# Attention stage of a two-layer time-mix and expert kernel: TensorE's order within a step changes, with ScalarE's and VectorE's after it

## The chip, the cores and the metric

The kernel runs on one core of one Trainium2 chip. Its five engines, TensorE (PE), VectorE (DVE), ScalarE (ACT), GpSimd (POOL) and the sync engine (SP), run their own instruction streams and meet at semaphores. The metric is the device time of the whole kernel in microseconds. Before the change it is 1264.72 us, the median of three runs (1261.82, 1264.72, 1269.57).

## The reference

The input `h` has 4 sequences of 2048 tokens with 256 features. Two time-mix layers run over it, then a residual sum is normalised, then a mixture of experts (8 experts, 2 per token) and another normalised sum follow.

```python
def _time_mix_layer(x, ln_w, ln_b, Wk, Wv, Wr, Wo):
    normed = _layer_norm(x, ln_w, ln_b)
    k = jnp.einsum('btd,ed->bte', normed, Wk)
    v = jnp.einsum('btd,ed->bte', normed, Wv)
    r = jax.nn.sigmoid(jnp.einsum('btd,ed->bte', normed, Wr))
    kv = k * v
    def step(state, kv_t):
        state = DECAY * state + (1.0 - DECAY) * kv_t
        return (state, state)
    _, states = jax.lax.scan(step, init, jnp.swapaxes(kv, 0, 1))
    y = r * jnp.swapaxes(states, 0, 1)
    return x + jnp.einsum('btd,ed->bte', y, Wo)
...
x = _layernorm(x + attention(x))      # both layers; the "finished rows"
gate_out = x @ Wg.T; top 2 of 8 experts, softmax over the two
x = _layernorm(x + sum of the two experts' gated MLPs, weighted)
```

## The kernel before, in words

The kernel has three phases: attention, experts, final normalisation. Only the attention phase is touched. It works on 16 chunks of 512 tokens (`CHUNKS`), each as 4 tiles of 128 tokens (`Q`). Features lie in two halves of 128 (`DC`). Every matrix product is made of three: high part by high part, high by low, low by high. So ScalarE writes a rounded high part of each operand (`x_hi`, `y_hi`) and VectorE or GpSimd the rest (`x_lo`, `y_lo`).

The phase is a software pipeline written out by hand. Each engine has a function `step(s, half, j)`, and in step s it holds four stages of different chunks: layer 1 of chunk s, layer 2 of chunk s-1, the end of the attention of chunk s-2 (residual sum `z`, its normalisation into `x1`), and the routing of chunk s-3 (transposes of the finished rows `x1`, the gate product, the choice of experts, the scatter of slots). `run` (L279 to L286) unrolls steps 0 to 5 and 14 to 19 and puts steps 6 to 13 in a hardware loop of two steps per pass. The order of the calls in `step` is the order of the instructions on the engine; nothing else schedules them. An instruction waits at the head of its engine's queue, and all behind it wait with it.

Names that matter:
- TensorE, `step` at L924: `project(l, s, n, e, j)` makes k, v and r of layer l for feature half e (6 groups of 6 matmuls for both halves); `rows2` transposes layer 2's normalised input `normed1` into the two banks `tp`; `output2` is layer 2's output product; `rows3` transposes finished rows `x1` into the same `tp`; `gates` multiplies them by the router's weights; `transpose(0, s + 1, ...)` is layer 1's input of the next chunk, again in `tp`. The two `tp` banks are shared by three users, so each of them waits until the last one has been read: `x_lo` (L638) for the layers' inputs, `keep_x1T` (L417) for the finished rows.
- ScalarE, `step` at L433: `normalize` (L382), `x_hi` (L389), `keep_k` (L395), `gate_r` (L402), `y_hi` (L409), `keep_x1T` (L417).
- VectorE, `step` at L770: `residual1` (L745), `norm_stats` (bn_stats L624, bn_aggr L630, `ve` L632, `nm` L633), `recur` (`kv` L685, the scan L692, the carry L695), `x_lo` (L638), `residual2` (`z`, L765, with its own `norm_stats`), `choose` (L705 to L722), `place` (up to the cast into `slot_u`, L737).
- GpSimd, `step` at L561: `rstd` (L532, L534) turns `ve` and `nm` into the factors of a normalisation, `gated` (L298) multiplies state and gate into `y`, `y_lo` (L305) is its low part, and the scatters (L78) are indirect DMAs that it issues, 8 per step from step 4 on. Its order is untouched.
- TensorE's last work in a step is layer 1's output product (L876 to L878) in two halves; the second one overwrites a bank from which `place` of the same step has to read first, so it waits for `slot_u`.

Of the kernel before, what the change touches and what calls it, by code (L numbers as in the profile page):

```python
# [41 lines left out]
DC = D // P  # L42
# [22 lines left out]
def at(s, n):  # L65

    return isinstance(s, int) and s == n
# [103 lines left out]
def attention_phase(nc, h, w_att, ln_wb, w_gate, w_ffn, x_src, x_acc, slot_list, kept):  # L171
    ident, w_raw_all, base, table = kept.ident, kept.w_raw, kept.base, kept.table
    pairs, slot_u, s_sc = kept.pairs, kept.slot_u, kept.s_sc
    with ExitStack() as ctx:
# [191 lines left out]
        def _(act):  # L366
# [38 lines left out]
            def y_hi(l, n, e):  # L405
                act.wait_ge(s_y[l], n * 2 + e + 1)
                if within(n, 1, CHUNKS):
                    act.wait_ge(s_po[l], n * 2)
                nc.scalar.activation(yh[l][:, e, :], y[l][:, e, :], ACT.Copy).then_inc(s_yh[l], 1)  # L409

            def keep_x1T(s):

                for dc in range(DC):
                    act.wait_ge(s_pt[2], s * 2 + dc - 5)
                    if within(s, 4, CHUNKS + 2):
                        act.wait_ge(s_g, s - 3)
                    nc.scalar.activation(x1T[:, dc, :], tp[dc][:, :], ACT.Copy).then_inc(s_x1T, 1)  # L417
# [15 lines left out]
            def step(s, half, j):  # L433
                layer1, layer2 = within(s, 0, CHUNKS - 1), within(s, 1, CHUNKS)
                if layer1:
                    for e in range(DC):
                        if e == 1 and layer2:
                            if within(s, 2, CHUNKS):
                                act.wait_ge(s_pt[1], s * 2 - 2)
                            normalize(1, xr, normed[1], s - 1, s_n[1])  # L440
                        if at(s, 0):
                            keep_k(0, s, e, j, None, 0)
                        elif at(s, 1):
                            keep_k(0, s, e, j, s_kv[0], 2)
                        else:
                            keep_k(0, s, e, j, s_kv[1], s * 2 + e - 3)
                        gate_r(0, s, e, j)
                elif layer2:
                    act.wait_ge(s_pt[1], s * 2 - 2)
                    normalize(1, xr, normed[1], s - 1, s_n[1])  # L450
                if at(s, 0):
                    x_hi(0, 1)
                if at(s, CHUNKS):
                    keep_x1T(s)
                if layer2:
                    x_hi(1, s - 1)
                if at(s, CHUNKS):
                    normalize3(s, half, j)
                if layer1:
                    for e in range(DC):  # L460
                        y_hi(0, s, e)
                if at(s, 0):
                    split_weights(1)
                    act.wait_ge(s_biassb[1], 2)
                if within(s, 3, CHUNKS + 2) and not at(s, CHUNKS) and not at(s, CHUNKS + 1):
                    keep_x1T(s)
                if within(s, 1, CHUNKS - 2):
                    act.wait_ge(s_pt[0], s * 2 + 2)
                    normalize(0, x_in[:, 1 - j, :, :], normed[0], s + 1, s_n[0])
                if layer2:  # L470
                    if at(s, CHUNKS):
                        keep_k(1, s - 1, 0, j, s_kv[1], 2 * s - 3)
                    else:
                        keep_k(1, s - 1, 0, j, s_kv[0], s * 2 + 1)
                if within(s, 2, CHUNKS + 1) and not at(s, CHUNKS):
                    normalize3(s, half, j)
                if layer2:
                    gate_r(1, s - 1, 0, j)
                if within(s, 1, CHUNKS - 2):
                    x_hi(0, s + 1)  # L480
                if layer2:
                    if at(s, CHUNKS):
                        keep_k(1, s - 1, 1, j, s_kv[1], 2 * s - 2)
                    else:
                        keep_k(1, s - 1, 1, j, s_kv[0], s * 2 + 2)
                    y_hi(1, s - 1, 0)
                if within(s, 3, CHUNKS + 2):
                    act.wait_ge(s_gap, s - 2)
                    if within(s, 5, CHUNKS + 2):
                        act.wait_ge(s_sc[1 - j], (half - 2 + j) * SCAT)  # L490
                    nc.scalar.activation(pairs[1 - j][:, :, 0, 1], gap[:, :], ACT.Sigmoid)
                    nc.scalar.activation(pairs[1 - j][:, :, 1, 1], gap[:, :], ACT.Sigmoid, scale=-1.0).then_inc(s_prob, 1)
                if layer2:
                    gate_r(1, s - 1, 1, j)
                    if at(s, CHUNKS):
                        keep_x1T(s + 1)
                    y_hi(1, s - 1, 1)
# [114 lines left out]
        def _(dve):  # L612
# [157 lines left out]
            def step(s, half, j):  # L770
                layer1, layer2 = within(s, 0, CHUNKS - 1), within(s, 1, CHUNKS)
                if layer2:
                    residual1(s, j)
                    norm_stats(1, xr, s - 1)
                    if not at(s, CHUNKS):
                        add_input(s, j)
                if at(s, CHUNKS):
                    residual2(s, j)
                if layer1:
                    for e in range(DC):  # L780
                        recur(0, s, e, j)
                if at(s, 0):
                    x_lo(0, 1)
                    keep_bias(1)
                    low_weights(1)
                if layer2:
                    x_lo(1, s - 1)
                if within(s, 1, CHUNKS - 2):
                    dve.wait_ge(s_x[1 - j], half * 16 + 16 * (1 + j))
                    norm_stats(0, x_in[:, 1 - j, :, :], s + 1)  # L790
                if at(s, CHUNKS):
                    add_input(s, j)
                if within(s, 2, CHUNKS + 1) and not at(s, CHUNKS):
                    residual2(s, j)
                if at(s, CHUNKS):
                    choose(s - 3)
                    for e in range(DC):
                        recur(1, s - 1, e, j)
                        gated(dve, 1, s - 1, e)
                        y_lo(dve, 1, s - 1, e)  # L800
                if within(s, 3, CHUNKS + 2) and not at(s, CHUNKS):
                    choose(s - 3)
                if layer2 and not at(s, CHUNKS):
                    recur(1, s - 1, 0, j)
                if within(s, 1, CHUNKS - 2):
                    x_lo(0, s + 1)
                if within(s, 3, CHUNKS + 2):
                    place(s - 3, half, j)
                if at(s, EARLY + 2):
                    dve.wait_ge(s_base, EARLY + 1)  # L810
                    big_table(nc, dve, kept)
                if layer2 and not at(s, CHUNKS):
                    recur(1, s - 1, 1, j)
# [5 lines left out]
        def _(pe):  # L819
# [104 lines left out]
            def step(s, half, j):  # L924
# [14 lines left out]
                if at(s, CHUNKS):  # L939

                    output2(s, j)
                    rows3(s, j, s_xl[0], 2 * s)
                    rows2(s, ((s_x1T, s * 2 - 4),))
                    gates(s, s_res, s * 2)
                    project(1, s, s - 1, 0, j)
                elif at(s, CHUNKS + 1):
                    rows3(s, j, s_xl[1], 2 * s - 2)
                    output2(s, j)
                    gates(s, s_slot, s - 3)
                elif at(s, CHUNKS + 2):  # L950
                    rows3(s, j, s_x1T, 2 * s - 6)
                    gates(s, s_slot, s - 3)
                else:
                    if layer2:
                        rows2(s, ((s_xl[0], s * 2 + 2),))
                    if within(s, 2, CHUNKS):
                        output2(s, j)
                    if within(s, 3, CHUNKS):
                        rows3(s, j, s_xl[1], s * 2)
                    if layer2:  # L960
                        project(1, s, s - 1, 0, j)
                    if at(s, 3):
                        pe.wait_ge(s_wg, 16)
                    if within(s, 3, CHUNKS):
                        gates(s, s_res, s * 2)
                if within(s, 1, CHUNKS - 2):
                    pe.wait_ge(s_n[0], s + 2)

                    if within(s, 1, 2) and isinstance(s, int):
                        pe.wait_ge(s_xl[1], 2 * s)  # L970
                    else:
                        pe.wait_ge(s_x1T, s * 2 - 4)
                    transpose(0, s + 1, normed[0])
                if layer2:
                    project(1, s, s - 1, 1, j, (0, 1))
# [569 lines left out]
```

## Time and profile before

| | |
|---|---|
| Median of three runs | 1264.72 us (1261.82 to 1269.57) |
| Profiled execution: its time, its span | 1267.21 us, 1265.4 us |
| Mean granted clock of TensorE | 0.956 |
| PE busy, share of the span | 1103.8 us, 87% |
| DVE | 926.9 us, 73% |
| POOL | 858.0 us, 68% |
| ACT | 656.5 us, 52% |
| PE busy from 30 to 440 us (attention) | 361.05 of 410.00 us |
| POOL busy there | 290.78 us |

Times are microseconds from the start of the span. The attention takes the first 555 us or so. A row of the time-ordered view is a start, a duration, the engine, the line of the kernel, the operation, and its output and inputs, with a count if several equal ones are merged; behind it in brackets stands how long the engine had been idle, and what released it.

### The profile page before, as it was taken

How to read it: one execution, taken by the hardware profiler on the slowest of the kernel's cores; microseconds unless marked ns; L12 is line 12 of the kernel's file. 1: busy time of each engine (PE TensorE's matmuls, PEld its weight loads, DVE VectorE, ACT ScalarE, POOL GpSimd, SP SyncE). 2: the span in 40 equal slices, each digit the busy share in tenths (PEclk: the TensorE clock that was granted, in tenths of full speed). 3: DMA queues.
4: the chain of work that ended last, by engine and by line, in shares of the span. 5: the costliest groups of instructions: out<-in, count | busy, mean ns of one | idle time of the engine just before them, and what ended most of it. 6: DMA issues, size and time to landing. Idle time of an engine off the chain costs nothing. (4 is left out here: it accounts for less than half of the span.)

```text
span 1265.4 us, 23767 instructions
## 1 busy us (share of the span) xinstructions
PE 1103.8 (87%) x7172; PEld 988.0 (78%) x7172; DVE 926.9 (73%) x1973; ACT 656.5 (52%) x1091; POOL 858.0 (68%) x696
## 2 busy tenths in 40 slices
PE   6899888988888889748999999999999999999910
PEld 5778777777777777636888888888889999999910
DVE  5678888888888887745776666666667888888737
ACT  4455555555455554324554454444555666566618
POOL 3355777777777777666666776666677676777634
PEclk9899999999999999859999999999999999999965
DMA  4011111111111111157656666656668898998559
GB/s 150 17 51 58 48 48 51 51 50 50 50 50 50 50 51 34 34 129 185 160 139 147 161 158 154 143 137 157 151 157 224 238 237 227 238 246 229 134 167 381
DMA packets 80662, 164.20 MB, mean 130 GB/s; under 512 B 27424, under 2 KB 45600, under 8 KB 80352
## 3 DMA queue, kind: packets, MB, share of 16 engines
q1 hardware_dynamic: 49248, 126.16, 31.8%
q0 software_dynamic: 31360, 37.38, 15.7%
q8 instruction: 26, 0.43, 0.2%
q14 instruction: 28, 0.23, 0.1%
HBM read 118.01 MB, written 45.49 MB: 129 GB/s over the span
## 5 line engine op out<-in xcount | busy, mean ns | idle before, releaser
L1163 POOL DMA_INDIRECT x_acc<-fy_sb,pair_out x142 | 284.7, 2005 | 152.9 <-DVE fy_sb L1264 76.9
L1319 PE MATMUL fring<-fxh,fw_hi 128*128 128x256 f32 (+1 forms) x816 | 265.3, 325 | 4.0 <-DVE fxl L1255 1.9
L1321 PE MATMUL fring<-fxh,fw_lo 128*128 128x256 f32 (+1 forms) x816 | 265.3, 325 | 0.0
L1320 PE MATMUL fring<-fxl,fw_hi 128*128 128x256 f32 (+1 forms) x816 | 265.0, 325 | 0.0
L1182 ACT ACTIVATE fw_hi<-w_raw 128x1024 fp32r<-128x1024 f32 x153 | 161.1, 1054 | 149.0 <-PE fy L1362 132.4
L1235 DVE TENSOR_TENSOR fw_lo<-w_raw,fw_hi 128x1024 fp32r<-128x1024 f32 x153 | 186.5, 1219 | 17.8 <-ACT fw_hi L1182 16.5
L88 POOL DMA_INDIRECT xg<-x_src,pair_in x142 | 159.8, 1125 | 43.3 <-issue 42.7
L78 POOL DMA_INDIRECT slot_list<-pairs,slot_u x128 | 140.1, 1095 | 47.6 <-issue 30.9
L1319 PEld LDWEIGHTS fring<-fxh,fw_hi 128*128 128x128 f32 x816 | 153.7, 188 | 18.0 <-issue 4.1
L1360 PE MATMUL fy<-fw_hi,gh 128*128 128x256 f32 x568 | 163.7, 288 | 0.9 <-issue 0.9
L1321 PEld LDWEIGHTS fring<-fxh,fw_lo 128*128 128x128 f32 x816 | 153.8, 189 | 13.3
L1320 PEld LDWEIGHTS fring<-fxl,fw_hi 128*128 128x128 f32 x816 | 153.8, 188 | 13.2
L865 PE MATMUL ring<-xh,w_hi 128*128 128x512 f32 x384 | 158.9, 414 | 3.1 <-DVE xl L638 2.9
L1362 PE MATMUL fy<-fw_hi,gl 128*128 128x256 f32 x568 | 159.5, 281 | 1.1 <-issue 1.1
L1361 PE MATMUL fy<-fw_lo,gh 128*128 128x256 f32 x568 | 159.5, 281 | 0.4 <-issue 0.4
L866 PE MATMUL ring<-xl,w_hi 128*128 128x512 f32 x384 | 153.4, 400 | 0.0
L867 PE MATMUL ring<-xh,w_lo 128*128 128x512 f32 x384 | 153.3, 399 | 0.0
L1244 DVE TENSOR_TENSOR gated<-fring,silu 128x512 f32<-128x512 f32 x142 | 98.2, 691 | 72.4 <-PE fring L1321 62.6
L1195 ACT ACTIVATE gh<-gated 128x512 fp32r<-128x512 f32 x142 | 89.6, 631 | 83.6 <-DVE gated L1244 77.9
L298 POOL TENSOR_TENSOR y<-state,r_sb 128x512 f32<-128x512 f32 x62 | 80.2, 1293 | 70.7 <-DVE state L692 67.0
L1361 PEld LDWEIGHTS fy<-fw_lo,gh 128*128 128x128 f32 x568 | 108.4, 191 | 1.2 <-issue 1.2
L409 ACT ACTIVATE yh<-y 128x512 fp32r<-128x512 f32 x64 | 40.5, 632 | 132.4 <-POOL y L298 131.8
(148 smaller groups left out, 2378.8 us busy)
## 6 DMA issues: line engine op xcount, KB each, us to landing
w_raw<-w_ffn SPq DMA_DIRECT2D x153, 512.0 KB
x_in<-h SPq DMA_DIRECT2D x16, 512.0 KB, 3.3
x_src<-x SPq DMA_DIRECT2D x16, 512.0 KB
x_acc<-x SPq DMA_DIRECT2D x16, 512.0 KB
acc<-x_acc SPq DMA_DIRECT2D x16, 512.0 KB, 7.7
out<-o SPq DMA_DIRECT2D x16, 512.0 KB, 6.8
xg<-x_src,pair_in POOLq DMA_INDIRECT x142
x_acc<-fy_sb,pair_out POOLq DMA_INDIRECT x142
```

Source lines behind the costliest of these rows:

```text
L88: nc.gpsimd.indirect_dma_start(kept.xg[j][:, q, :], None, x_src, bass.IndirectOffsetOnAxis(kept.pair_in[j][:, q, 0:1].bitcast(U32), 0)).th ...
L865: nc.tensor.matmul(out, hi, xh[l][:, dc, :], start=dc == 0, stop=False)
L866: nc.tensor.matmul(out, hi, xl[l][:, dc, :], start=False, stop=False)
L1163: nc.gpsimd.indirect_dma_start(x_acc, bass.IndirectOffsetOnAxis(pair_out[j][:, q, 0:1].bitcast(U32), 0), y[j][:, q, :], None, compute_op=A ...
L1182: nc.scalar.activation(w_hi[:, j, low:high], w_raw[:, j, low:high], ACT.Copy).then_inc(s_whi[i], 1)
L1235: nc.vector.tensor_tensor(w_lo[:, j, low:high], w_raw[:, j, low:high], w_hi[:, j, low:high].bitcast(F32), ALU.subtract).then_inc(s_wlo[i], 1)
L1319: nc.tensor.matmul(out, hi, rows_hi, start=dc == 0, stop=False)
L1320: nc.tensor.matmul(out, hi, rows_lo, start=False, stop=False)
L1321: last = nc.tensor.matmul(out, lo, rows_hi, start=False, stop=dc == DC - 1)
L1360: nc.tensor.matmul(out, a, hi, start=hc == 0, stop=False)
L1361: nc.tensor.matmul(out, a, lo, start=False, stop=False)
L1362: last = nc.tensor.matmul(out, c, hi, start=False, stop=hc == HC - 1)
```

## The change

It reorders calls in three of the `step` functions and adjusts the waits that protect the shared `tp` banks. No instruction is added or taken away. In steps 3 to 15 TensorE's order behind layer 1's projections was: layer 2's transposes, layer 2's output, finished rows' transposes, layer 2's projections of the first half, gates. It becomes: finished rows' transposes, layer 2's output, layer 2's transposes, gates, layer 2's projections of the first half. In steps 1 and 2, which have no finished rows to transpose, the output (step 2) comes ahead of the transposes. On ScalarE the copies of the finished rows come ahead, and the two `y_hi` of layer 1 stand around layer 2's `x_hi`. On VectorE layer 2's `x_lo` moves behind `norm_stats` of the next chunk of layer 1.

```diff
--- before.py
+++ after.py
@@ -450,19 +450,20 @@
                     normalize(1, xr, normed[1], s - 1, s_n[1])
                 if at(s, 0):
                     x_hi(0, 1)
-                if at(s, CHUNKS):
+                if within(s, 3, CHUNKS):
                     keep_x1T(s)
+                if layer1:
+                    y_hi(0, s, 0)
                 if layer2:
                     x_hi(1, s - 1)
                 if at(s, CHUNKS):
                     normalize3(s, half, j)
                 if layer1:
-                    for e in range(DC):
-                        y_hi(0, s, e)
+                    y_hi(0, s, 1)
                 if at(s, 0):
                     split_weights(1)
                     act.wait_ge(s_biassb[1], 2)
-                if within(s, 3, CHUNKS + 2) and not at(s, CHUNKS) and not at(s, CHUNKS + 1):
+                if at(s, CHUNKS + 2):
                     keep_x1T(s)
                 if within(s, 1, CHUNKS - 2):
                     act.wait_ge(s_pt[0], s * 2 + 2)
@@ -783,11 +784,11 @@
                     x_lo(0, 1)
                     keep_bias(1)
                     low_weights(1)
-                if layer2:
-                    x_lo(1, s - 1)
                 if within(s, 1, CHUNKS - 2):
                     dve.wait_ge(s_x[1 - j], half * 16 + 16 * (1 + j))
                     norm_stats(0, x_in[:, 1 - j, :, :], s + 1)
+                if layer2:
+                    x_lo(1, s - 1)
                 if at(s, CHUNKS):
                     add_input(s, j)
                 if within(s, 2, CHUNKS + 1) and not at(s, CHUNKS):
@@ -951,25 +952,25 @@
                     rows3(s, j, s_x1T, 2 * s - 6)
                     gates(s, s_slot, s - 3)
                 else:
-                    if layer2:
-                        rows2(s, ((s_xl[0], s * 2 + 2),))
+                    if within(s, 3, CHUNKS):
+                        rows3(s, j, s_xl[0], s * 2 + 2)
                     if within(s, 2, CHUNKS):
                         output2(s, j)
-                    if within(s, 3, CHUNKS):
-                        rows3(s, j, s_xl[1], s * 2)
                     if layer2:
-                        project(1, s, s - 1, 0, j)
+                        if within(s, 3, CHUNKS):
+                            rows2(s, ((s_x1T, s * 2 - 4),))
+                        else:
+                            rows2(s, ((s_xl[0], s * 2 + 2),))
                     if at(s, 3):
                         pe.wait_ge(s_wg, 16)
                     if within(s, 3, CHUNKS):
                         gates(s, s_res, s * 2)
+                    if layer2:
+                        project(1, s, s - 1, 0, j)
                 if within(s, 1, CHUNKS - 2):
                     pe.wait_ge(s_n[0], s + 2)
 
-                    if within(s, 1, 2) and isinstance(s, int):
-                        pe.wait_ge(s_xl[1], 2 * s)
-                    else:
-                        pe.wait_ge(s_x1T, s * 2 - 4)
+                    pe.wait_ge(s_xl[1], s * 2)
                     transpose(0, s + 1, normed[0])
                 if layer2:
                     project(1, s, s - 1, 1, j, (0, 1))
```

TensorE in one pass of the loop, behind layer 1's projections. The names in square brackets are the semaphores waited for. Before:

```order
L823 MATMUL tp<-ident,normed 128x128 [waits xl_ready0,normed_1]
L823 MATMUL tp<-ident,normed 128x128 x7
L876 MATMUL ring<-w_hi,yh 128x256 [waits r_ready0,yl_ready1,yh_ready1]
...
L823 MATMUL tp<-ident,x 128x128 [waits xl_ready1,x1_ready]
L823 MATMUL tp<-ident,x 128x128 x7
L865 MATMUL ring<-xh,w_hi 128x512 [waits kv_ready0,xl_ready1,xh_ready1]
...
L912 MATMUL out_0<-wg,x1T 128x8 [waits residual_ready,x1T_ready]
L912 MATMUL out_0<-wg,x1T 128x8 x7
L823 MATMUL tp<-ident,normed 128x128 [waits x1T_ready,normed_0]
```

And with the change, where line numbers are one higher:

```order
L824 MATMUL tp<-ident,x 128x128 [waits xl_ready0,x1_ready]
L824 MATMUL tp<-ident,x 128x128 x7
L877 MATMUL ring<-w_hi,yh 128x256 [waits r_ready0,yl_ready1,yh_ready1]
...
L824 MATMUL tp<-ident,normed 128x128 [waits x1T_ready,normed_1]
L824 MATMUL tp<-ident,normed 128x128 x7
L913 MATMUL out_0<-wg,x1T 128x8 [waits residual_ready,x1T_ready]
L913 MATMUL out_0<-wg,x1T 128x8 x7
L866 MATMUL ring<-xh,w_hi 128x512 [waits kv_ready0,xl_ready1,xh_ready1]
...
L824 MATMUL tp<-ident,normed 128x128 [waits xl_ready1,normed_0]
```

The finished rows' transposes (`tp<-ident,x`) and the output have changed places with layer 2's transposes (`tp<-ident,normed`, waiting for normed_1), and the gates (out_0<-wg,x1T) now stand ahead of layer 2's projections.

VectorE in the second step of the loop's pass, from layer 1's carry to the statistics of `z`. Before:

```order
L695 COPY carry<-state 128x1
L638 TENSOR_TENSOR xl<-tp,xh 128x512 x2
L624 BN_STATS stats<-x_in 128x6 x4
L630 BN_AGGR mv<-stats 128x2 x4
L632 TENSOR_SCALAR ve<-mv 128x4
L633 TENSOR_SCALAR nm<-mv 128x4
L765 TENSOR_TENSOR z<-ring,u 128x512 x2
L624 BN_STATS stats<-z 128x6 x4
```

With the change:

```order
L696 COPY carry<-state 128x1
L625 BN_STATS stats<-x_in 128x6 x4
L631 BN_AGGR mv<-stats 128x2 x4
L633 TENSOR_SCALAR ve<-mv 128x4
L634 TENSOR_SCALAR nm<-mv 128x4
L639 TENSOR_TENSOR xl<-tp,xh 128x512 x2
L766 TENSOR_TENSOR z<-ring,u 128x512 x2
L625 BN_STATS stats<-z 128x6 x4
```

`xl` of layer 2 has moved behind the five groups of the next chunk's statistics and stands directly ahead of `z`.

## Rows read from the trace of the kernel before

**Rows 1.** TensorE's waits from 119 to 476 us: total, times, longest (us).

```profile
PE out L876 <- DVE slot_u L737: 17.4, 11, 1.9
PE tp L823 <- DVE xl L638: 16.1, 11, 1.6
PE tp L823 <- ACT normed L382: 13.2, 10, 1.8
```

**Rows 2.** Time order, TensorE in step 12: start, duration, operation, idle time before.

```profile
378.62 0.39 PE L865 MATMUL ring<-xh,w_hi 128*128 128x512 f32 x1
...
388.93 1.10 PE L823 MATMUL tp<-ident,normed 128*128 128x128 f32 x8 [1.73 <-ACT normed L382]
...
394.49 1.06 PE L823 MATMUL tp<-ident,x 128*128 128x128 f32 x8 [1.59 <-DVE xl L638]
395.31 0.48 PE L865 MATMUL ring<-xh,w_hi 128*128 128x512 f32 x1
...
399.69 1.85 PE L912 MATMUL out<-wg,x1T 128*128 128x8 f32 x16
...
410.24 0.38 PE L876 MATMUL out<-w_hi,yh 128*128 128x256 f32 x1 [1.84 <-DVE slot_u L737]
```

**Rows 3.** Time order, VectorE in step 12.

```profile
379.86 1.29 DVE L745 TENSOR_TENSOR xr<-out,x_in 128x512 f32<-128x512 f32 x2 [0.43 <-issue]
...
393.05 1.29 DVE L638 TENSOR_TENSOR xl<-tp,xh 128x512 fp32r<-128x512 f32 x2
394.26 1.40 DVE L624 BATCH_NORM_STATS2 stats<-x_in 128x6 f32<-128x256 f32 x4
...
396.24 1.23 DVE L632 TENSOR_SCALAR ve<-mv 128x4 f32<-128x4 f32 x1
...
408.55 1.64 DVE L737 CAST slot_u<-slot_f 128x8 uint32<-128x8 f32 x1
```

**Rows 4.** Time order, GpSimd in step 12.

```profile
394.89 1.29 POOL L298 TENSOR_TENSOR y<-state,r_sb 128x512 f32<-128x512 f32 x1
396.14 1.29 POOL L305 TENSOR_TENSOR yl<-y,yh 128x512 fp32r<-128x512 f32 x1
...
401.43 1.05 POOL L532 TENSOR_TENSOR rs<-ve,neg_half 128x4 f32<-128x4 f32 x1
...
408.88 1.27 POOL L305 TENSOR_TENSOR yl<-y,yh 128x512 fp32r<-128x512 f32 x1
```

**Rows 5.** Time order, VectorE in step 15, `ve` of z and the gates' first reader.

```profile
493.71 1.32 DVE L632 TENSOR_SCALAR ve<-mv 128x4 f32<-128x4 f32 x1
...
497.64 0.19 DVE L705 COPY g<-out 128x32 f32<-128x32 f32 x1 [2.55 <-PE out L912]
```

**Rows 6.** Time order, GpSimd in step 15, two products in a row.

```profile
492.44 2.54 POOL L305 TENSOR_TENSOR yl<-y,yh 128x512 fp32r<-128x512 f32 x2
```

**Rows 7.** Time order, TensorE in steps 1, 2 and 3.

```profile
50.15 0.48 PE L865 MATMUL ring<-xh,w_hi 128*128 128x512 f32 x1 [2.91 <-DVE xl L638]
...
76.61 0.48 PE L865 MATMUL ring<-xh,w_hi 128*128 128x512 f32 x1 [0.21 <-issue]
...
82.24 1.09 PE L823 MATMUL tp<-ident,normed 128*128 128x128 f32 x8 [1.18 <-ACT normed L382]
...
104.83 0.47 PE L865 MATMUL ring<-xh,w_hi 128*128 128x512 f32 x1
```

**Rows 8.** Time order, GpSimd's `yl` of layer 1, steps 1, 2 and 3.

```profile
49.96 1.29 POOL L305 TENSOR_TENSOR yl<-y,yh 128x512 fp32r<-128x512 f32 x1
...
76.45 1.29 POOL L305 TENSOR_TENSOR yl<-y,yh 128x512 fp32r<-128x512 f32 x1
...
103.80 1.28 POOL L305 TENSOR_TENSOR yl<-y,yh 128x512 fp32r<-128x512 f32 x1
```

**Rows 9.** Stretches: bounds, length, each engine's busy time, PEclk (granted clock), DMA share, GB/s.

```profile
33.00:38.00 5.00, 5.00 (x26) 4.94 (x25) 2.44 (x4) 0.00 (x0) 0.00 (x0) 0.57 0.00 0
50.00:56.00 6.00, 5.86 (x19) 4.62 (x20) 1.98 (x11) 2.98 (x6) 3.71 (x5) 0.72 0.00 0
```

## The prediction

> **What bounds the kernel now.** The views were read in this order: the page, the waits of TensorE in the attention stage, then the time-ordered rows of TensorE, VectorE and GpSimd for single steps. Only the attention stage changes, in its steps 1 to 15, so the question is what sets the length of a step there. Three waits stop TensorE once per step, together 46.7 us over 11 steps: for layer 2's normalised rows, for the low parts of layer 2's input (`xl`), and for the slots [rows 1]. The change is aimed at the first two. Whether they are worth anything depends on the third, because a wait that ends later in the same step takes up what the earlier ones give back.
>
> Step 12 is the step I work out; it starts at 378.62, with its first matmul, and ends some 1.5 us after the slots. TensorE waits 1.73 us for the normalised rows, 1.59 for `xl`, and 1.84 for the slots [rows 2]. The slots come from VectorE (the cast of slot_u, which ends at 408.55 + 1.64 = 410.19 [rows 3]). So the step ends by a chain VectorE, GpSimd, ScalarE, VectorE, in which TensorE has 1.84 us of spare time. The reader is to see that GpSimd is nearly always at work there, and that some VectorE operations do not run beside it: `ve`, four elements per partition, takes 1.23 us and ends at 397.47, where GpSimd's `yl` ends at 396.14 + 1.29 = 397.43 [rows 3, 4]. In step 15 `ve` takes 1.32 us, to 495.03, and two products of GpSimd in a row end at 494.98 [rows 5, 6]. The cast of the slots starts 0.33 us before a product of GpSimd at 408.88 and ends 0.04 after it [rows 3, 4]. I read this as a hold: VectorE waits until GpSimd pauses, and a GpSimd instruction that follows on the last without a gap keeps it.
>
> **The change, part by part, in steps 4 to 14 (11 steps).**
> TensorE's reordering. The transposes of finished rows and the output now stand ahead of the transposes of layer 2, so 394.49 - 1.59 - 388.93 = 3.97 us of work lie where the 1.73 us wait was, and that wait is covered. Its price is nothing, and so would be its gain as long as the slots end the step.
>
> VectorE's reordering. `x_lo` of layer 2 (two subtractions, 1.29 us as a pair [rows 3]) moves behind norm_stats of the next chunk. Its statistics start at 393.05 instead of 394.26, and `ve` at 393.05 + (396.24 - 394.26) = 395.03. At that moment GpSimd's product `y` runs (394.89 to 396.18) and `yl` follows from 396.14 without a gap [rows 4]. If the hold works as above, `ve` ends at 397.47 as before: the 1.2 us that it started earlier are lost. `x_lo` then runs where `z` stood, from 397.45 to 398.74, and TensorE's projections of layer 2 start at 398.8 instead of 395.31, 3.5 us later. The gates, 1.7 us (their row's 1.85 [rows 2], less the last one's overlap with what follows), now stand ahead of them, so the net delay of TensorE is 1.8 us, which its 1.84 us of spare time just pays. The cost falls elsewhere: `z`, its statistics and its `ve` come 1.2 us later. GpSimd used that `ve` at 401.43 without having waited [rows 4], so part of the 1.2 is hidden; bounds for the slots are 0 and 1.2 us, and I take 0.5, since the `yl` at 408.88 that the cast waits for hangs on two parallel chains, of which one only moves.
>
> TensorE's clock. The idle times of a step, now 1.7 and 1.6 us, become one: the wide matmuls, the moved output included, are done by 388.93 - 1.73 + 3.97 = 391.2, the transposes and gates by 393.7 (0.82 and 1.7 us), and the projections start at 398.8, after 5.1 us of nothing [rows 2]. In the trace of before the granted clock was 0.72 over 6.0 us after the 2.91 us wait of step 1, and 0.57 over 5.0 us after another wait at the start of the stage [rows 7, 9]; that is the 1.2 GHz level for part of the time, and a loss of 6.0 x 0.28 = 1.7 us and 5.0 x 0.43 = 2.15 us. I expect such a fall in most steps and take 1.9 us each. TensorE then ends the step, 1.9 us late. But most of this comes back: when TensorE ends a step, VectorE's next step, whose first addition now starts 1.24 us after the step does [rows 3], starts up to 1.2 to 1.7 us earlier against it, and with it all that TensorE waits for later. What stays is between 0.5 us (the slots' chain alone) and 1.0 (a fall that costs 2.4). I take 0.6: 11 x 0.6 = **6.6 us**.
>
> ScalarE's reordering puts the two copies of x1T ahead and layer 2's `x_hi` between the two `y_hi`. The wait for GpSimd's product that `y_hi` has there covers them, and a 5.1 us wait of TensorE covers a late `x_hi`. Without that cover the price would be a pair of such operations, 1.29 us as VectorE's pair, a step. I take nothing.
>
> **Steps 1 to 3.** Here GpSimd has no scatters, a step is shorter, and TensorE is close to being the bound. `ve` lands inside a `yl` of GpSimd in each of them. Step 1: that `yl` ends at 49.96 + 1.29 = 51.25 [rows 8]; `nm` and `x_lo` follow, to about 52.7, and TensorE, which started at 50.15, starts at 52.75: **+2.6**. Step 2: `yl` ends at 77.74, `x_lo` at 79.2, the projections start at 79.3 instead of 76.61, and the 1.18 us wait at 82.24 absorbs part [rows 7, 8]: 1.5, plus 1.9 for a fall of the clock, since this idle time gets about as long as the 2.91 us one of step 1: **+3.4**. Step 3: `yl` ends at 105.08 [rows 8], projections at 106.5 instead of 104.83, less 1.7 for the gates moved ahead: 0 without a fall of the clock, 2 with one; **+1.0**.
>
> **Step 15.** It has no norm_stats of a next chunk, and `x_lo` stays where it was. The gates come earlier than the projections, and VectorE waits 2.55 us for them [rows 5]. Bounds 0 and -2.55; I take **-1.5**, because the projection that follows is needed too.
>
> Sum: 6.6 + 2.6 + 3.4 + 1.0 - 1.5 = +12.1 us. The stages after the attention do not change. Against the profiled execution (span 1265.4, time 1267.21) that is 1279.3; it lies 2.5 us above the median of the three runs (1264.72), and against that the sum is **1277 us**, my prediction, 1.0% slower. Less than 1% (12.6 us) is about what cannot be told from no change.
>
> **A rule weighed against the rows.** Everything above hangs on `ve` losing twice, to `y` and then to `yl`. The rows show `ve` of steps 12 and 15 losing to a product that began at nearly the same moment, and the cast losing to one that began later [rows 3 to 6]. The Trainium skill, SBUF — State Buffer, section "A bandwidth-pool intuition that's wrong (but worth ruling out)", has the port pair of VectorE and GpSimd as an exclusive lock, and the blocked side as going on about 115 ns after the holder's end. The trace agrees on the lock; read strictly, the rule lets `ve` in between `y` and `yl`, and the sum by it would be the first rival's.
>
> **The rivals.**
> 1. *`ve` is let in between `y` and `yl`.* It ends at about 396.3, `x_lo` at 397.7, and `z` starts 0.2 us later than before: nothing in steps 4 to 14, and the clock's fall is paid by the spare time. Steps 1 to 3 keep their +7.0 and step 15 its -1.5: +5.5, 1270 us. For it: the products are two instructions with a boundary. Against it: the cast that started 0.33 us before its product and lost. Chance 0.25.
> 2. *The other side: faster.* If `ve` reaches the port before `y` does, at 394.89, it is not held: in step 12 it comes 0.14 us too late, and that is the point which decides. `x_lo` would then end at 396.4, TensorE would start at 396.5 with the gates behind it, 0.5 us ahead of now, and `nm`, `z` and the slots' products would come up to 1.2 us earlier. At 0.65 us a step that gives -7, with 3 lost in steps 1 to 3 and -1.5 in step 15: -5.5, 1259 us; with all 1.2 us a step, -12. Against it: `ve` and `y` both follow the same scan of VectorE at fixed distances, so the 0.14 us repeat from step to step. Chance 0.07.
> 3. *The clock costs more.* If each fall costs 2.4 us or more and VectorE's lead does not make up for it, steps 4 to 14 lose 1.1 to 1.5 us each, and steps 1 to 3 lose 9: about +20, 1285 us. For it: the clock fell after both of the long waits shown, and the new wait is longer than either [rows 7, 9]. Chance 0.15.
>
> My own case has 0.53. Nearly half of it lies over +12.6 us.
>
> **Numbers.** Slower by over 1%: 0.53 x 0.45 + 0.15 = 0.39, rounded to 0.40. Faster by over 1% needs nearly the most that rival 2 can give, and I leave 0.07 for it and for what I have not seen. Within 1%: 0.53. The range goes from 1262, which cuts off most of rival 2, to 1287, a little over rival 3.
>
> **What would show it.** In the changed kernel's trace: no wait of TensorE for layer 2's normalised rows; a wait of 4 to 5.5 us before layer 2's first projection, put down to `xl`; `ve` of the next chunk's statistics taking 2 us or more, up to the end of `yl`; a lower granted clock over the attention stage than now; steps 4 to 14 longer by some 0.6 us; step 1 longer by 2.6. If `ve` takes 0.2 us, rival 2 holds; if it takes 1.3, rival 1. The prediction is wrong if the slots' chain gets shorter by a way that I have priced at nothing, ScalarE's order above all.

## The result, and the profile after

The changed kernel takes **1282.99 us** in the median (1281.87 to 1286.32, 4 runs), the kernel before 1263.27 in the same comparison (4 runs). The ratio is 1.0149, 95% interval 1.0118 to 1.0179: slower by 1.5%. The forecast was 1277, range 1262 to 1287. The profiled run took 1281.92.

From the page of the changed kernel, its span and its busy times:

```profile
span 1280.2 us, 23759 instructions
PE 1118.7 (87%) x7172; PEld 1008.4 (79%) x7172; DVE 932.2 (73%) x1973; ACT 662.0 (52%) x1091; POOL 863.0 (67%) x696
```

Its waits in steps 4 to 14, the first row TensorE's only one there (total, times, longest):

```profile
PE ring L866 <- issue: 47.0, 11, 4.7
```
```profile
DVE slot L730 <- PE out L986: 11.2, 11, 1.4
```

Against [rows 1]: three waits of TensorE, 46.7 us together, have become one of 47.0. The view puts it down to "issue" and not to `xl`; that `xl` ends it is seen in the rows of single steps. TensorE did not gain any time by the merger. The second row is new: VectorE now waits for TensorE's ranks of the tokens (L986) before it can make the slots, so TensorE ends the step.

Time order in step 12 of the changed kernel (it starts at 394.82): TensorE, VectorE, GpSimd.

```profile
407.00 1.03 PE L824 MATMUL tp<-ident,normed 128*128 128x128 f32 x8
407.87 1.85 PE L913 MATMUL out<-wg,x1T 128*128 128x8 f32 x16
414.10 0.77 PE L866 MATMUL ring<-xh,w_hi 128*128 128x512 f32 x1 [4.38 <-issue]
```
```profile
395.17 1.29 DVE L746 TENSOR_TENSOR xr<-out,x_in 128x512 f32<-128x512 f32 x2 [0.43 <-PE out L879]
...
410.35 2.38 DVE L633 TENSOR_SCALAR ve<-mv 128x4 f32<-128x4 f32 x1
412.65 0.16 DVE L634 TENSOR_SCALAR nm<-mv 128x4 f32<-128x4 f32 x1
412.72 1.28 DVE L639 TENSOR_TENSOR xl<-tp,xh 128x512 fp32r<-128x512 f32 x2
413.92 1.27 DVE L766 TENSOR_TENSOR z<-ring,u 128x512 f32<-128x512 f32 x2
```
```profile
410.21 1.27 POOL L298 TENSOR_TENSOR y<-state,r_sb 128x512 f32<-128x512 f32 x1
411.43 1.27 POOL L305 TENSOR_TENSOR yl<-y,yh 128x512 fp32r<-128x512 f32 x1
```

The reader is to see the lock in these three fences. `y` begins 0.14 us before `ve`; `yl` follows it at once and ends at 411.43 + 1.27 = 412.70; `ve`, four elements per partition, begins at 410.35 and ends at 412.73. It lost to both. `xl` ends at 414.00, and the projections of layer 2 start 0.1 us later.

The stretches around the wait, for [rows 9] (columns as there), first the idle one and then most of the eighteen projections:

```profile
408.70:414.10 5.40, 1.02 (x11) 0.96 (x10) 5.20 (x13) 0.65 (x2) 4.80 (x6) 0.84 0.01 0
414.10:419.10 5.00, 5.00 (x12) 3.94 (x13) 4.40 (x26) 2.88 (x6) 3.70 (x6) 0.50 0.01 0
```

At 0.50, the 1.2 GHz level, a projection matmul takes 0.43 us instead of 0.23. The eighteen take 420.68 - 414.10 = 6.6 us; before they took 431.97 + 0.23 - 427.76 = 4.4 in step 13. The whole of steps 4 to 14 ran at a granted clock of 0.90 after and 1.00 before:

```profile
125.00:497.00 372.00, 325.00 (x1850) 279.37 (x1849) 303.48 (x807) 185.97 (x352) 274.04 (x254) 0.90 0.13 47
```
```profile
119.00:476.00 357.00, 310.33 (x1851) 261.67 (x1850) 295.20 (x804) 182.28 (x352) 273.62 (x253) 1.00 0.14 49
```

**Where the time went**, from the starts of the steps in both traces:

| | before | after | difference | forecast |
|---|---|---|---|---|
| steps 4 to 14 | 356.9 | 371.9 | +15.1 | +6.6 |
| step 1 | 26.4 | 29.6 | +3.2 | +2.6 |
| step 2 | 26.3 | 30.1 | +3.8 | +3.4 |
| step 3 | 28.9 | 27.8 | -1.1 | +1.0 |
| step 15, to layer 2's output behind it | 35.1 | 32.9 | -2.2 | -1.5 |

Together +18.8, beside 19.7 between the medians. The spans differ by 14.8 only: what follows the attention took 3.7 us longer in the profiled run of before, which lay above its median.

### The profile page after: what moved, and what is told of

It reads as the page before. It is cut to its first block and busy times, and to the rows that moved or that the text cites. A ratio compares the mean times of both kernels' runs of the same rounds, so it can differ in the third digit from the quotient of the medians.

```text
span 1280.2 us, 23759 instructions
## 1 busy us (share of the span) xinstructions
PE 1118.7 (87%) x7172; PEld 1008.4 (79%) x7172; DVE 932.2 (73%) x1973; ACT 662.0 (52%) x1091; POOL 863.0 (67%) x696
## 5 line engine op out<-in xcount | busy, mean ns | idle before, releaser
L1164 POOL DMA_INDIRECT x_acc<-fy_sb,pair_out x142 | 292.4, 2059 | 142.2 <-DVE fy_sb L1265 78.4
L866 PE MATMUL ring<-xh,w_hi 128*128 128x512 f32 x384 | 169.0, 440 | 55.5 <-issue 50.1
L867 PE MATMUL ring<-xl,w_hi 128*128 128x512 f32 x384 | 163.4, 425 | 0.0
L868 PE MATMUL ring<-xh,w_lo 128*128 128x512 f32 x384 | 162.5, 423 | 0.0
L866 PEld LDWEIGHTS ring<-xh,w_hi 128*128 128x128 f32 x384 | 80.2, 209 | 73.9 <-issue 56.7
L1196 ACT ACTIVATE gh<-gated 128x512 fp32r<-128x512 f32 x142 | 89.6, 631 | 83.6 <-DVE gated L1245 83.6
L1250 DVE TENSOR_TENSOR gl<-gated,gh 128x512 fp32r<-128x512 f32 x142 | 97.3, 685 | 15.4 <-ACT gh L1196 15.4
```

What stands on the lines that cost most here:

```text
L866: nc.tensor.matmul(out, hi, xh[l][:, dc, :], start=dc == 0, stop=False)
L867: nc.tensor.matmul(out, hi, xl[l][:, dc, :], start=False, stop=False)
L868: last = nc.tensor.matmul(out, lo, xh[l][:, dc, :], start=False, stop=dc == DC - 1)
L1164: nc.gpsimd.indirect_dma_start(x_acc, bass.IndirectOffsetOnAxis(pair_out[j][:, q, 0:1].bitcast(U32), 0), y[j][:, q, :], None, compute_op=A ...
```

## The experiments

The theory: the time is lost by one swap, VectorE's `x_lo` behind norm_stats, because `ve` is held through `y` and `yl`; TensorE pays with a wait, and then with its clock. The rivals: TensorE's new order costs by itself; the clock costs nothing that the slots' chain would not cost; the hold is something else. Times are medians, with the kernel before in the same batch.

**Undo VectorE's part in the changed kernel** (e1_xlo_back).

```diff
+                if layer2:
+                    x_lo(1, s - 1)
                 ...
                     norm_stats(0, x_in[:, 1 - j, :, :], s + 1)
-                if layer2:
-                    x_lo(1, s - 1)
```

> The changed kernel with VectorE's order alone undone: layer 2's x_lo stands ahead of norm_stats of the next chunk again; TensorE's and ScalarE's new orders stay. My reading (hold): x_lo no longer waits behind ve, TensorE finds xl ready about when the gates end, its wait of 4.4 us a step and the fall of the clock (2.1 us) are gone, steps 4 to 14 fall from 33.8 to about 32.3 us, steps 1 to 3 and 15 gain some 3 us over before: 1258 us, range 1252 to 1264. Rival (TensorE's new order itself costs, for instance through the shared tp banks): stays over 1272. Rival (the slots' chain is untouched and nothing else moves): 1263, as before the change.

Measured: 1258.98 (before 1261.45), ratio 0.999 (0.9974 to 1.0005). All of the loss is gone, by this one swap. The granted clock is 1.00 again from 125 to 480 us. TensorE's waits, 125 to 520 us:

```profile
PE out L877 <- DVE slot_u L738: 15.7, 11, 1.5
PE tp L824 <- ACT normed L382: 13.4, 11, 1.3
PE ring L866 <- DVE z L766: 7.6, 10, 0.9
```

The long wait for `xl` is gone here and nothing clear of the noise is gained: the slots end the step, as in [rows 1]. In the two profiled runs steps 4 to 14 take 352.1 us instead of 356.9 and steps 1 to 3 take 83.6 instead of 81.6. So TensorE's and ScalarE's orders cost nothing, and are worth little at most.

**Only VectorE's part, in the kernel before** (e3_dve_only).

> The kernel before with VectorE's reordering alone: x_lo of layer 2 behind norm_stats of the next chunk, TensorE and ScalarE as before. Hold theory: x_lo ends 4.2 us later, TensorE keeps its wait for the normalised rows and waits about 5 us for xl with the gates still behind it, the clock falls: 35.5 us a step instead of 32.4, +34 in steps 4 to 14 and +5 in steps 1 to 3: 1295 to 1307. Rival (the lateness comes from TensorE's new order, in which layer 2's transposes are later): under 1270.

Measured: 1340.34 (before 1261.45), ratio 1.0624 (1.0607 to 1.064), 33 us above the top of what was expected. From 125 to 520 us:

```profile
PE tp L823 <- DVE xl L638: 58.4, 10, 6.1
```
```profile
DVE g L705 <- PE out L912: 57.5, 10, 6.5
```

In TensorE's old order the gates stand behind the projections that wait for `xl`. So each of the two engines waits for the other: TensorE 6 us for `xl`, then VectorE 6 us for the gates, whose copy is the head of its work on slots. I had priced only the first. The change's new order of TensorE is what keeps VectorE's swap from costing four times as much.

**`x_lo` between the statistics and `ve`** (e2_ve_behind_xlo): norm_stats calls it after its aggregation.

```diff
+                if between is not None:
+                    between()
                 ...
-                    norm_stats(0, x_in[:, 1 - j, :, :], s + 1)
-                if layer2:
+                    norm_stats(0, x_in[:, 1 - j, :, :], s + 1, lambda: x_lo(1, s - 1))
+                elif layer2:
                     x_lo(1, s - 1)
```

> The changed kernel with x_lo of layer 2 between the bn_aggr and the ve and nm of the next chunk's statistics, so that x_lo stands behind the same statistics but not behind the operation that GpSimd holds. Hold theory: x_lo starts 2.4 us earlier, TensorE's wait falls from 4.4 to about 2 us, ve is held all the same but by less; steps 4 to 14 about 32.4 to 32.8 us; 1265 to 1270 us. Rival (x_lo is late because the statistics themselves, 2 us of work, stand ahead of it, and the hold only takes time that VectorE would have spent waiting): within 4 us of the changed kernel's 1283.

Measured: 1259.18 (before 1261.45), ratio 0.9977 (0.9967 to 0.9988), better than expected. The statistics and their aggregation, 2.0 us together, may stand ahead of `xl`. `ve` takes 1.34 to 1.37 us in steps 6 to 13, against a `yl` alone, and stands behind `xl`; TensorE's wait halves:

```profile
PE ring L868 <- issue: 23.0, 11, 2.5
PE out L879 <- DVE slot_u L740: 4.9, 8, 0.8
```

What costs is thus the 2.4 us hold between the statistics and `xl`, not the distance that `xl` was moved. The clock still falls here (granted 0.93 from 125 to 480 us), and the time does not show it: the slots have again become what TensorE waits for in most steps, so that fall is paid out of spare time.

**Keep TensorE busy in the wait** (e4_filler): 14 matmuls of no use ahead of the projections, in steps 4 to 14.

```diff
+                        if within(s, 4, CHUNKS - 2):
+                            pe.wait_ge(s_kv[0], s * 2 + 2)
+                            for i in range(14):
+                                nc.tensor.matmul(bank(1, 0, 0, j), w_hi[:, 0, 0, 0:P], w_hi[:, 0, 0, 0:CH], start=True, stop=True)
```

> The changed kernel with 14 matmuls of 128x512 more (3.3 us) ahead of layer 2's first projection in steps 4 to 14, into the bank that this projection then overwrites: the wait for xl stays, but TensorE works through most of it. If the clock's fall costs time on the path: the first projections take 4.5 us instead of 6.6, TensorE stops being the last of the step or nearly, and the step goes from 33.8 to about 33.0 us, the slots' chain: 1272 to 1277. If the fall is paid by idle time anyway: 1283 within 3 us, and the slots or the rank product show the same 1.2 us of waiting.

Measured: 1273.36 (before 1261.45), ratio 1.01 (1.0083 to 1.0117). As expected, the steps get shorter: 33.7 and 32.7 us by turns in steps 8 to 13, instead of 33.9 to 34.1. The clock stays at 1.00, and the slots end the step again:

```profile
125.00:480.00 355.00, 335.29 (x1959) 284.24 (x1958) 298.62 (x791) 178.33 (x343) 268.61 (x249) 1.00 0.13 47
```
```profile
PE out L877 <- DVE slot_u L738: 4.9, 10, 0.7
```

1282.99 - 1273.36 = 9.6 us come back, of 19.7 (7.8 if each is taken against the kernel before in its own batch; steps 4 to 14 alone go from 371.9 to 362.1 us in the two traces). So much the fall of the clock costs, as far as one can tell by filling the wait. The rest is no longer TensorE's delay, since it waits for `slot_u` again; there VectorE's hold, 2.42 to 2.60 us here, stands ahead of `z` and the slots.

**Undo it in steps 1 to 3 only** (e5_early_steps).

> The changed kernel with x_lo of layer 2 ahead of norm_stats in steps 1 to 3 alone. It measures what the early steps lost, 6.0 us between the two traces (steps 1 and 2 longer by 3.2 and 3.8, step 3 shorter by 1.1): 1275 to 1278 us. If the early loss is made up later anyway, because steps 4 onward are a cycle of their own: over 1280.

Measured: 1277.99 (before 1263.99), ratio 1.0113 (1.0089 to 1.0137). 5 us come back (5.7 against the kernel before in each batch), of the 5.9 that the table shows for these steps. Where GpSimd has no scatters the wait also appears, and is put down to `xl`: TensorE, VectorE and GpSimd in step 1 of the changed kernel, for [rows 7, 8]:

```profile
52.37 0.77 PE L866 MATMUL ring<-xh,w_hi 128*128 128x512 f32 x1 [5.38 <-DVE xl L639]
```
```profile
50.49 0.51 DVE L633 TENSOR_SCALAR ve<-mv 128x4 f32<-128x4 f32 x1
```
```profile
49.71 1.27 POOL L305 TENSOR_TENSOR yl<-y,yh 128x512 fp32r<-128x512 f32 x1
```

`ve` ends 0.02 us after that `yl`.

**Is it the lock?** One can ask for the same numbers in another form. In e6_single_elements all `ve` and `nm` of the changed kernel become four operations of one element each, in e7_before_single those of the kernel before.

```diff
-                nc.vector.tensor_scalar(ve[i][:, :], mv[i][:, :, 1], EPS, None, ALU.add).then_inc(s_ve[i], 1)
+                for q in range(Q):
+                    last = nc.vector.tensor_scalar(ve[i][:, q:q + 1], mv[i][:, q, 1:2], EPS, None, ALU.add)
+                last.then_inc(s_ve[i], 1)
```

> The changed kernel, VectorE's order and all, with each ve and nm written as four operations of one element per partition instead of one of four. Nothing moves, only the form of the held operations changes. Hold theory with the form as its condition: the small ones are not held by GpSimd, x_lo of layer 2 starts 1.8 us earlier, TensorE's wait falls to about 2.5 us: 1258 to 1265 us. If GpSimd holds every operation of VectorE that stands there, or the time was lost otherwise: 1283, or more by the 6 extra operations of some 0.07 us each per statistic.

> The kernel before with ve and nm written as single elements. There ve is held 1.2 us in each of steps 4 to 14, but what the held time delays (z, the second statistics) had spare time ahead of GpSimd. Slots' chain theory: within 0.3% of before, 1258 to 1262. If VectorE's held time was on the path there too: 1.2 us less in 11 steps, 1249.

Measured: 1278.43 and 1280.15 (before 1263.99), ratios 1.0115 (1.0093 to 1.0137) and 1.0137 (1.0112 to 1.0163). Both missed by 13 us and more. But the form works. VectorE and GpSimd in e6:

```profile
373.13 0.34 DVE L634 TENSOR_SCALAR ve<-mv 128x1 f32<-128x1 f32 x4
```
```profile
373.00 1.28 POOL L298 TENSOR_TENSOR y<-state,r_sb 128x512 f32<-128x512 f32 x1
```

Four operations in 0.34 us while `y` runs: no hold. What the kernels lost instead is in steps 8, 10 and 12 (steps 8 to 13 are 35.2 and 33.1 us by turns in e6), each the first step of a pass of the loop, where VectorE stands for 3.1 to 4.4 us before its first addition, released by nothing that the profile shows. From e7's time order (70 us, two steps, apart) and from its page:

```profile
255.60 1.29 DVE L749 TENSOR_TENSOR xr<-out,x_in 128x512 f32<-128x512 f32 x2 [4.41 <-issue]
...
325.71 1.29 DVE L749 TENSOR_TENSOR xr<-out,x_in 128x512 f32<-128x512 f32 x2 [4.00 <-issue]
...
394.77 1.29 DVE L749 TENSOR_TENSOR xr<-out,x_in 128x512 f32<-128x512 f32 x2 [3.73 <-issue]
```
```profile
q14 instruction: 45, 0.37, 0.1%
```

This queue, which brings instructions, had 28 packets in the kernel before. The loop body had become longer by 36 VectorE instructions a pass, and I read the waits as instructions fetched; that reading was only tested by making the addition smaller, in the next run.

**Single elements for the next chunk's statistics alone** (e9_single_next_chunk), the edit of e6 under `if i == 0`.

> The changed kernel with ve and nm as single elements only in the statistics of the next chunk of layer 1, the ones in question: 6 more VectorE instructions a step instead of 18. In the two kernels with 18 more, one step in two grew by 4 us in a wait of VectorE that no engine ends, at the start of each pass of the loop, and more instruction bytes were loaded. If that is the longer code: here both steps of a pass take 32.0 to 32.4 us, and the total is 1260 to 1266 us. If the small form itself costs in every second step, 1272 to 1278 again.

Measured: 1264.19 (before 1262.94), ratio 1.0005 (0.9979 to 1.0032); 29 packets, and steps 8 to 13 are 31.5 to 32.8 us long, so no step has grown by 4 us. VectorE's order is that of the changed kernel, and only the form of two small operations differs: 18.8 us less than 1282.99. With e1 and e2 this shows the hold of `ve` as the cause, twice by the place and once by the form. TensorE's wait is shorter, not gone (and the granted clock is 0.93 from 125 to 480 us, as in e2):

```profile
PE ring L872 <- issue: 28.4, 11, 3.1
```

**The slots' cast.** If the slots end the step, their chain is where time is to be had, and the cast there is held as `ve` is. In e10, e12, e13 and e8 the reduction writes the integers itself:

```diff
-                link(m, 6, nc.vector.reduce_sum(slot_f[:, :, :], own[:, :, :, :], AX_X))
-                nc.vector.tensor_copy(slot_u[1 - j][:, :, :], slot_f[:, :, :].rearrange("p c q -> p q c")).then_inc(s_slot, 1)
+                nc.vector.reduce_sum(slot_u[1 - j][:, :, :].rearrange("p q c -> p c q"), own[:, :, :, :], AX_X).then_inc(s_slot, 1)
```

e8_no_cast has it with e1's order and e6's single elements.

> VectorE's order undone as in the 1259 us kernel, ve and nm as single elements, and the slots written by the reduction itself, without the cast of 8 elements that GpSimd holds 1.2 to 1.5 us at the end of each step. The slots end the step, so their being 1.3 us earlier should shorten it: 31.0 us a step instead of 32.2 in steps 4 to 14, 1243 to 1250 us. If the product that held the cast ends the step by another way (yl itself, or the next additions): 1257 to 1260.

Measured: 1264.58 (before 1263.99), ratio 1.0005 (0.9989 to 1.002). A miss, with e6's waits again: steps of 31.1 to 31.3 us alternate with steps of 35.2 to 36.5.

e10_before_no_cast is the kernel before with that edit alone.

> The kernel before with the slots written by the reduction, without the cast that GpSimd holds. Slots' chain theory: the slots end each step, and the hold of the cast costs 1.2 to 1.5 us, of which the step gets 1.0: 31.4 us instead of 32.4 in steps 4 to 14, 1249 to 1253 us. If TensorE's other waits or VectorE's next additions take it up: within 3 us of before.

Measured: 1256.25 (before 1262.94), ratio 0.9939 (0.9918 to 0.9959), about half of what was expected. The slots' wait is gone and the next one in line has grown:

```profile
PE tp L823 <- ACT normed L382: 22.1, 12, 2.0
PE tp L823 <- DVE xl L638: 8.9, 6, 1.6
PE out L876 <- DVE slot_u L737: 0.7, 4, 0.2
```

These are the waits that TensorE's new order covers. e12_ve_behind_no_cast is e2, e13_xlo_back_no_cast is e1, each with the edit.

> The kernel with layer 2's x_lo between bn_aggr and ve (1259 us), and the slots written by the reduction. It has the changed kernel's order on TensorE and ScalarE and neither of the two holds on a path that ends the step: 30.8 to 31.2 us in steps 4 to 14, 1245 to 1250 us. Rival: TensorE's wait for xl and the fall of the clock, 2.1 us each, now end the step instead of the slots: 1256 to 1259.

> TensorE's and ScalarE's order of the changed kernel, VectorE's order undone, and the slots written by the reduction; no instruction more than before. TensorE has no long wait here, so no fall of the clock, and neither hold ends the step. If the clock's fall was what bounded the 1251 us kernel: 31.0 us a step instead of 31.35, 1246 to 1249 us. If the later chain over GpSimd and VectorE bounds both: 1250 to 1254.

Measured: e12 1251.11 (before 1262.94), ratio 0.989 (0.9855 to 0.9925), just above what was expected; e13 **1248.97** (before 1264.38), ratio 0.988 (0.9856 to 0.9904), within what was expected. e13 is better than both kernels, by 1.2% and by 34 us. Its steps take 31.3 to 31.5 us, and its waits from 125 to 480 us are:

```profile
PE tp L824 <- ACT normed L382: 11.4, 11, 1.3
PE ring L866 <- issue: 4.9, 11, 0.6
PE ring L866 <- DVE z L766: 4.6, 6, 0.9
```

TensorE's order was worth nothing clear of the noise while the slots ended the step (e1). With ScalarE's it is worth some 7 us once they do not (e10 against e13; the two intervals, each against the kernel before in its own batch, do not meet).

## Why the prediction was right, and which terms were off

The mechanism held where it was put. **The hold**: `ve` through `y` and `yl`, forecast as "2 us or more", was 2.37 to 2.54 us in each of steps 4 to 14. Rival 1, which let `ve` in between the two, and rival 2, which needed 0.14 us of luck, did not happen; the 0.14 us did repeat (0.13 to 0.15 us in steps 7 to 12). **TensorE's wait**: 4 to 5.5 us forecast, 4.4 and 4.0 in steps 12 and 13, 4.3 in the mean of the eleven steps, with 3.3 and 3.7 as the shortest. **Steps 1 and 2** and **step 15** came within 0.7 us each; in **step 3** it was -1.1 instead of +1.0: the clock did not fall (the new wait was 0.33 us), and the two waits that this step had before, 0.96 and 0.27 us, are gone, which I had not priced.

The term that failed is **steps 4 to 14**, 1.37 us each instead of 0.6. The total is within the range in part by luck: this term alone was 8.5 us too low, steps 1 and 2 another 1.0, and steps 3 and 15 gave 2.8 back. Three parts of it:

1. *"Most of this comes back"*, VectorE's lead of 1.2 to 1.7 us. VectorE gained 1.24 - 0.35 = 0.9 us on TensorE in step 12 and 0.82 - 0.22 = 0.6 in step 13, by the start of `xr` in the step. An operand bounds it, the ranks. The rows at the end of step 12 of the changed kernel, TensorE, VectorE and GpSimd (step 13 starts at 428.94):

```profile
424.48 0.24 PE L986 MATMUL out<-picked,ones 128*128 128x8 bf16 x4
...
428.94 0.40 PE L866 MATMUL ring<-xh,w_hi 128*128 128x512 f32 x1
```
```profile
424.76 0.19 DVE L730 TENSOR_TENSOR slot<-out,base 128x32 f32<-128x32 f32 x1 [1.23 <-PE out L986]
425.07 1.01 DVE L732 TENSOR_TENSOR own<-sel,slot 128x64 f32<-128x64 f32 x1
...
429.16 1.29 DVE L746 TENSOR_TENSOR xr<-out,x_in 128x512 f32<-128x512 f32 x2
```
```profile
424.68 1.30 POOL L305 TENSOR_TENSOR yl<-y,yh 128x512 fp32r<-128x512 f32 x1
```

In each of steps 4 to 14 `slot` starts 0.28 us after the ranks do, and TensorE's step ends 4.18 us after `slot` starts. VectorE comes to its next `xr` in 4.40 us here, and in 4.53 a step earlier; in the kernel before these were 4.96 and 5.23. So most of what VectorE gained is that its own chain behind the ranks got shorter, and a TensorE that is late by more makes the ranks late by as much. (The 0.43 us idle before `xr` in step 12 is put down to PE's `out`, but the same 0.43 us stood there in the kernel before, put down to "issue" [rows 3].) The projections started at 19.3 us of the step, which is my 20.2 less 0.9.

2. *The clock*, 1.9 us a step: 6.6 us instead of 4.4 for the eighteen projections is 2.2 in step 12, and the filler run returned 9.6 us over 11 steps. It is nearer to the rival of the costlier clock, whose total of 1285 us was nearer than mine too; its condition, a fall of 2.4 us or more, was not met, but "VectorE's lead does not make up for it" was.

3. *Only one step was worked out.* In the kernel before the steps take 33.2 and 32.15 us by turns, in the changed kernel 34.1 and 33.9. Step 12 is of the long kind. It lost 1.0 us, which was the upper bound of my range; step 13 lost 1.8. Its spare time at the slots had been 1.47 us and not 1.84 [rows 2], which explains 0.4 of the difference. The mean of one pair is the 1.37. From the start of its projections to its end, step 13 takes 15.0 us, before it took 16.2.

One gain I had not seen, and it is smaller than it looks. In the changed kernel the slots' cast is not held; first after, then before, from 125 and 119 to 480 us:

```profile
L738 DVE CAST slot_u<-slot_f x10: 171/172/172, 156.4 to 460.2; 128x8 uint32<-128x8 f32 x10
```
```profile
L737 DVE CAST slot_u<-slot_f x11: 1421/1504/1661, 148.2 to 473.0; 128x8 uint32<-128x8 f32 x11
```

But the hold has only moved, to `own`, two instructions ahead of the cast in the same chain, which now stands beside `yl` (425.07 to 426.08 against 424.68 to 425.98 in step 12, above). After and before, steps 4 to 14:

```profile
L732 DVE TENSOR_TENSOR own<-sel,slot x11: 802/1006/1647, 155.3 to 492.9; 128x64 f32<-128x64 f32 x11
L731 DVE TENSOR_TENSOR own<-sel,slot x11: 215/215/218, 147.7 to 472.5; 128x64 f32<-128x64 f32 x11
```

From the start of `slot` to the end of the cast it is 0.5 us less in the mean of the eleven steps (1.94 instead of 2.45). With TensorE's delay gone (e1, e2) `own` takes 0.2 us and the cast 1.3 to 1.5 once more. A hold is a matter of phase: whoever moves one of the two engines moves all its holds.

One reading of mine was weaker than I put it: "the cast that started 0.33 us before its product and lost", the argument against rival 1. [Rows 4] leave out what GpSimd was doing at 408.55 in the kernel before:

```profile
407.85 1.00 POOL L78 DMA_INDIRECT slot_list<-pairs,slot_u  x1 [0.16 <-issue]
```

All eleven casts start 0.07 to 0.33 us before the end of such a scatter, so the end of the scatter may have held them until the product began. Which of the two it was, no run here settles.

## What to carry to other kernels

A small VectorE operation that GpSimd can hold off belongs behind what other engines wait for, not ahead of it; how many products GpSimd has in a row then sets its price, not its size. A lead that an engine gains ends at the first operand that the other engine makes last, so look for that operand before booking the lead. Where steps alternate, work out one of each kind; and a wait that is covered pays only after the wait behind it, here the slots, is gone.

## What the runs showed of the hardware

- The lock between VectorE and GpSimd is not handed over between two GpSimd instructions that follow on each other: an operation that takes 0.17 us took 2.38, and ended 0.03 us after the second. The Trainium skill, SBUF — State Buffer, section "A bandwidth-pool intuition that's wrong (but worth ruling out)", gives about 115 ns after the holder's end, measured the other way round, with VectorE holding off GpSimd. After the last of a row the trace is within 0.1 us of that; between the two `ve` was not let in.
- The same four numbers per partition as four one-element operations ran in 0.34 us beside a running product, and a reduction that writes integers took 0.22 us where reduction and cast had taken 1.9 (0.22 + 1.64 in step 12 of before).
- After a wait of 4.4 us TensorE's granted clock was 0.50 for the next 5.0 us, while it had nothing but matmuls to do; with 14 matmuls in the wait it stayed at 1.00.
- 36 more VectorE instructions in a loop pass of two steps cost a wait of 3.7 to 4.4 us in each of the three passes shown, released by nothing in the profile, and brought the instruction packets from 28 to 45. With 12 more there were 29 packets and no such wait. Where between them the cost sets in, and whether it is the fetching of instructions, these runs do not settle.
